# One stage for the item schedule and the projection of a graph-attention layer with a mixture-of-experts layer behind it

## What is computed

```python
xn = layernorm(x)
x_l = xn @ W_l + b_l                    # "left": rows gathered by src
x_r = xn @ W_r + b_r                    # "right": rows of the dst node
g = leaky_relu(x_r[dst] + x_l[src], 0.2)
alpha = softmax over edges of a dst of (sum_c g * att + log(edge_weight))
x = x + segment_sum(x_l[src] * alpha, dst) + bias
x = x + experts(layernorm(x))           # top 2 of 8, 256 -> 512 -> 256, gelu
```

## Time and profile before

| | us |
|---|---|
| median of 3 runs | 2044.14 |
| the profiled execution, its own time | 2046.96 |
| its span, first to last instruction | 2045.2 |
| constants | 0 to 5.1 |
| schedule | 5.1 to 111.4 |
| projection, with the start of its block | 111.4 to 224.1 |
| edges and all that follows | 224.1 to 2045.2 |

### The profile page before, as it was taken

The page is one execution under the profiler, slowest core; times in us unless marked ns, Lnnn a source line. Parts: engine busy times, 40 slices in busy tenths (PEclk is TensorE's granted clock), DMA queues, the critical chain, the costliest instruction groups (busy, mean ns, idle before and its releaser), DMA issues. The chain is left out here.

```text
span 2045.2 us, 41611 instructions
## 1 busy us (share of the span) xinstructions
PE 1732.4 (85%) x9503; PEld 1464.5 (72%) x9504; DVE 1504.5 (74%) x2831; ACT 1225.6 (60%) x3096; POOL 1236.6 (60%) x1364
## 2 busy tenths in 40 slices
PE   0079679999999999999999999998587999999960
PEld 0068457777777778778787787886486999999950
DVE  1956478988988989889899898998877333333325
ACT  0021258898988989889898898998450323333310
POOL 0457577777777767777777777771517555555520
PEclk9999789999999999999999999999658999999985
DMA  5257677777777778777787777871741222222229
GB/s 169 36 192 259 202 244 230 236 231 222 237 229 231 236 218 239 228 234 234 222 241 230 234 234 225 244 237 55 256 162 42 65 69 72 69 71 70 70 72 337
DMA packets 220914, 377.54 MB, mean 185 GB/s; under 512 B 46120, under 2 KB 104720, under 8 KB 220576
## 3 DMA queue, kind: packets, MB, share of 16 engines
q1 hardware_dynamic: 146056, 205.58, 31.0%
q0 software_dynamic: 53760, 150.08, 26.5%
q10 hardware_dynamic: 20936, 20.41, 2.9%
HBM read 321.55 MB, written 55.59 MB: 184 GB/s over the span
## 5 line engine op out<-in xcount | busy, mean ns | idle before, releaser
L713 POOL DMA_INDIRECT rows<-left_rows,idx x896 | 850.9, 950 | 314.2 <-issue 301.9
L1051 PE MATMUL p_row<-rights,hotT 128*128 128x256 f32 x1792 | 516.7, 370 | 49.2 <-DMA rows<-left_rows,idx 23.8
L1053 PE MATMUL p_row<-rows,ident 128*128 128x256 f32 x1792 | 539.8, 383 | 0.0
L1114 PE MATMUL p_gain<-W,hots 128*128 128x264 f32 x1792 | 487.1, 396 | 34.5 <-ACT W L1021 20.7
L1114 PEld LDWEIGHTS p_gain<-W,hots 128*128 128x128 f32 x1792 | 325.9, 190 | 127.3 <-issue 68.6
L1051 PEld LDWEIGHTS p_row<-rights,hotT 128*128 128x128 f32 x1792 | 329.9, 192 | 115.5 <-issue 33.1
L940 ACT ACTIVATE L<-p_row 128x512 f32<-128x512 f32 x448 | 263.3, 588 | 111.7 <-PE p_row L1053 110.5
L1010 ACT ACTIVATE far<-iota_row,dl 128x128 f32<-128x128 f32 x896 | 305.0, 391 | 0.0
L876 DVE TENSOR_TENSOR W<-rows,p_weights 128x1024 f32<-128x1024 f32 x224 | 271.7, 1213 | 42.4 <-PE p_gain L1114 41.9
L785 DVE TENSOR_TENSOR L<-L,p_weights 128x1024 f32<-128x1024 f32 x224 | 270.8, 1209 | 37.8 <-ACT L L940 33.9
L1540 ACT ACTIVATE e_hT<-e_ph,b_column 128x128 f32<-128x128 f32 x420 | 119.7, 368 | 267.6 <-PE e_ph L1565 267.6
(11 more groups left out here) (240 smaller groups left out, 1906.8 us busy)
## 6 DMA issues: line engine op xcount, KB each, us to landing
rights<-right_rows SPq DMA_DIRECT2D x448, 256.0 KB
locals<-item_locals SPq DMA_DIRECT2D x112, 256.0 KB, 3.7
rows<-left_rows,idx POOLq DMA_INDIRECT x896
right_rows<-p_parts SPq DMA_DIRECT2D x50, 256.0 KB, 2.0
c_rows<-results SPq DMA_DIRECT2D x12, 1024.0 KB, 13.4
w<-in_L_ffn_W SPq DMA_DIRECT2D x16, 512.0 KB, 6.6
left_rows<-p_y SPq DMA_DIRECT2D x50, 132.0 KB, 1.8
kept_rows<-X ACTq DMA_DIRECT2D x50, 128.0 KB, 2.0
```

The lines of the kernel that those rows point to most:

```text
L713: nc.gpsimd.indirect_dma_start(out=rows[:, g.slot(RINGS), n, :], out_offset=None, in_=d["left"][:, :], in_offset=bass.IndirectOffsetOnAxis ...
L1051: nc.tensor.matmul(to, hotT[:, g.slot(2), i, :], rights[:, g.slot(2), n, part * D:(part + 1) * D], start=(part == 0), stop=False)
L1053: last = nc.tensor.matmul(to, s["ident"][:, :], rows[:, g.slot(RINGS), i, 0:D], start=False, stop=True)
L1114: last = nc.tensor.matmul(p_gain[:, n, 0:D + H], hots[:, g.slot(2), i, :], W[:, g.slot(2), i, :, :].rearrange("p h c -> p (h c)"), start=( ...
```

## The change

`schedule` and `project` become one block, `prepare`. What it does:

- x comes on SP's queue in four pieces (tiles 0 to 6, 7 to 20, 21 to 34, 35 to 48); the block ends are read straight from the input `dst` right behind the first piece, 391 and 390 elements; ACT's queue loads `att`, weights and biases first and then copies the three edge tables to DRAM.
- Statistics, roots and reciprocals are taken by seven tiles (b = 0 to 6) and not all at once. 49 tiles are projected and not 50; the padding tile of `right` is stored as zeros.
- Normalizing moves from DVE to ACT, the copy of `left` out of PSUM too. The biases of left and right enter PSUM by a two-row matmul ahead of each product (a float32r row of ones against the high and low part of the bias), so DVE adds none. DVE takes both the high and the low part of `right` out of PSUM; POOL is left with the output bias.
- Each step of the schedule stands between two tiles of the projection, in the written order of its engine: the searches at DVE's tiles 2 to 8, the gathers behind POOL's tile 8, the steps after the gather at tiles 22 to 41.
- Rows of x are kept by seven tiles in one store on SP's queue, and not one tile at a time on ACT's.
- All loops are written out.

The added lines, cut to their core (indentation cut by twelve columns; the removed lines are the two functions printed above). In order: POOL, SP, PE, ACT, DVE.

```diff
+PIECES = ((0, BY), (BY, 3 * BY), (3 * BY, 5 * BY), (5 * BY, 7 * BY))
...
+    pool.wait_ge(weights_in, 96)
+    for t in range(NODE_TILES):
+        pool.wait_ge(normed, t + 1)
+        nc.gpsimd.tensor_tensor(X[:, t, :], X[:, t, :], bias_out[:, :], ALU.add).then_inc(residual, 1)
+        if t == 8:
+            pool.wait_ge(items_done, 1)
+            pool.wait_ge(padded, 16 * 6)
+            for q in range(QI):
+                for i, (rows, table) in enumerate(((rows_d, "dst"), (rows_s, "src"), (rows_w, "weight"))):
+                    nc.gpsimd.indirect_dma_start(
+                        out=rows[:, q, :], out_offset=None, in_=d[table][:, :],
+                        in_offset=bass.IndirectOffsetOnAxis(ap=t_idx[:, q:q + 1], axis=0),
+                    ).then_inc(gathered[i], 16)
+        if t == 26:
+            pool.wait_ge(local_done, 1)
+            nc.gpsimd.tensor_copy(local16[:, :, :], local[:, :, :]).then_inc(local_kept, 1)
...
+    def load_x(i):
+        sp.dma_start(X[:, a:own, :], x[a * P:own * P, :].rearrange("(t p) f -> p t f", p=P)).then_inc(x_in[i], 16)
+            sp.dma_start(X[0:N - full * P, full, :], x[full * P:N, :]).then_inc(x_in[i], 16)
...
+    load_x(0)
+    for i, at, blocks in ((0, 0, EB), (1, PAIR * P - 1, EB - 1)):
+        sp.dma_start(ends[:, i, 0:blocks], dst[at:at + (blocks - 1) * PAIR * P + 1][::PAIR * P]
+                     .rearrange("(a b) -> a b", a=1), allow_slow_non_contiguous=True).then_inc(ends_in, 16)
+    for i in range(1, len(PIECES)):
+        load_x(i)
+    sp.wait_ge(pads_set, 6)
+    for side in range(2):
+        sp.dma_start(d["right"][NODE_TILES * P:NT * P, side * D:(side + 1) * D], X[:, NODE_TILES, :]).then_inc(stored, 16)
+    for t in range(NODE_TILES):
+        sp.wait_ge(left_done, t + 1)
+        sp.dma_start(d["left"][t * P:(t + 1) * P, :], y[:, t % 4, :]).then_inc(tile_stored[t % 4], 16)
+        sp.wait_ge(right_done, t + 1)
+        sp.dma_start(d["right"][t * P:(t + 1) * P, :], parts[:, t % 4, :, :].rearrange("p a f -> p (a f)")
+                     ).then_inc(tile_stored[t % 4], 16)
+        if t == 12:
+            sp.wait_ge(items_done, 1)
...
+            sp.wait_ge(local_done, 2)
...
+            sp.wait_ge(stored, 16 * 5)
...
+            sp.wait_ge(local_kept, 1)
...
+        if t == 41:
+            for kind in range(MARKS):
+                sp.wait_ge(breaks_done, kind + 1)
...
+        if t % BY == BY - 1:
+            b = t // BY
+            sp.wait_ge(residual, (b + 1) * BY)
+            sp.dma_start(d["kept"][b * BY * P:(b + 1) * BY * P, :].rearrange("(t p) f -> p t f", p=P),
+                         X[:, tiles_of(b), :]).then_inc(rows_kept, 16)
+    sp.wait_ge(stored, 16 * (6 + MARKS))
+    sp.wait_ge(rows_kept, 16 * BATCHES)
+    for k in range(4):
+        sp.wait_ge(tile_stored[k], 32 * len(range(k, NODE_TILES, 4)))
...
+    def multiply(t):
+        pe.wait_ge(x_turned_copied, t + 1)
+        wait(pe, left_done, t - 1)
+        wait(pe, right_done, t - 1)
+        for side, (at, wide) in enumerate(((0, DL), (DL, D))):
+            nc.tensor.matmul(py[:, t % 2, side, 0:wide], both_ones[:, :], bias_parts[:, at:at + wide], start=True, stop=False)
+            for h in range(KD):
+                last = nc.tensor.matmul(py[:, t % 2, side, 0:wide], xT[:, t % 2, h * P:(h + 1) * P],
+                                        W[:, h, side, 0:wide], start=False, stop=(h == KD - 1))
+        last.then_inc(projected, 1)
...
+    turn(0)
+    pe.wait_ge(columns_done, 2)
+    for t in range(NODE_TILES):
+        if t + 1 < NODE_TILES:
+            turn(t + 1)
+        multiply(t)
+        if t == 1:
+            pe.wait_ge(ends_done, 1)
+            for a in range(2):
+                last = nc.tensor.matmul(ps[:, a, 0:EB], s["ones"][0:1, :], offs[0:1, a, :], start=True, stop=True)
+            last.then_inc(spread, 1)
+        i = t - 26
+        if 0 <= i < 3 * QI:
+            pe.wait_ge(local_done, 1 if i < QI else 3)
+            if i >= 2:
+                pe.wait_ge(turned_copied, i - 1)
+            if i >= 2 * QI:
+                pe.wait_ge(weights_done, 1)
+            from_ = local if i < QI else sf if i < 2 * QI else rows_w
+            nc.tensor.transpose(ps[:, i % 2, 0:P], from_[:, i % QI, :], s["ident"][:, :]).then_inc(turned, 1)
...
+    act.dma_start(attb[:, :], att.rearrange("h c -> (h c)").partition_broadcast(P)).then_inc(weights_in, 16)
+        act.dma_start(W[:, :, i, 0:D], w.rearrange("(k p) f -> p k f", p=P)).then_inc(weights_in, 16)
+    for at, b in ((0, b_l), (DL, b_r)):
+        act.dma_start(bias_rows[:, at:at + D], b.partition_broadcast(2)).then_inc(weights_in, 16)
+    act.dma_start(bias_out[:, :], bias.partition_broadcast(P)).then_inc(weights_in, 16)
+    for k, a in (("dst", dst), ("src", src), ("weight", edge_weight)):
+        act.dma_start(flat[k][0:E].rearrange("(a b) -> a b", a=16),
+                      a.rearrange("(a b) -> a b", a=16)).then_inc(padded, 16)
...
+    def norm(t):
+        act.wait_ge(scaled, t // BY + 1)
...
+        nc.scalar.activation(xn[:, t % 2, :], X[:, t, :], ACT.Identity, bias=shift[:, t:t + 1],
+                             scale=std[:, 2, t:t + 1]).then_inc(normed, 1)
...
+    def copy_left(t):
+        act.wait_ge(projected, t + 1)
+        wait(act, tile_stored[t % 4], 32 * (t // 4))
+        nc.scalar.activation(y[:, t % 4, :], py[:, t % 2, 0, 0:DL], ACT.Copy).then_inc(left_done, 1)
+    root(0)
+    for t in range(-2, NODE_TILES):
+        if t + 2 < NODE_TILES:
+            norm(t + 2)
+        if 0 <= t + 1 < NODE_TILES:
+            copy_turned(t + 1)
+        if t >= 0:
+            copy_left(t)
+        if (t + 4) % BY == 0 and 0 < t + 4 < NODE_TILES:
+            root((t + 4) // BY)
+        if t == 31:
+            act.wait_ge(floored, 1)
+            nc.scalar.activation(rows_w[:, :, :], rows_w[:, :, :], ACT.Ln).then_inc(logged, 1)
+        i = t - 27
+        if 0 <= i < 3 * QI:
+            act.wait_ge(turned, i + 1)
+            to = (s["dl"], s["srcs"], s["logw"])[i // QI][:, (i % QI) * P:(i % QI + 1) * P]
+            nc.scalar.activation(to, ps[:, i % 2, 0:P], ACT.Copy).then_inc(turned_copied, 1)
...
+    def take_stats(b):
+        for i, (a, z) in enumerate(PIECES):
+            if a <= b * BY < z:
+                v.wait_ge(x_in[i], 32 if z > full else 16)
...
+        nc.vector.tensor_scalar(std[:, 0, tiles_of(b)], mv[:, tiles_of(b), 1], EPS, None, ALU.add).then_inc(sqrt_ready, 1)
...
+    def scale(b):
+        v.wait_ge(sqrt_done, b + 1)
+        step(nc.vector.reciprocal(std[:, 2, tiles_of(b)], std[:, 1, tiles_of(b)]))
+        nc.vector.scalar_tensor_tensor(shift[:, tiles_of(b)], mv[:, tiles_of(b), 0], -1.0, std[:, 2, tiles_of(b)],
...
+    def take_parts(t):
+        v.wait_ge(projected, t + 1)
+        wait(v, tile_stored[t % 4], 32 * (t // 4))
+        right = py[:, t % 2, 1, 0:D]
+        nc.vector.tensor_scalar(parts[:, t % 4, 0, :].bitcast(I32), right.bitcast(I32),
+                                LOW_BITS, LOW_BITS, ALU.logical_shift_right, ALU.logical_shift_left).then_inc(right_high, 1)
+        v.wait_ge(right_high, t + 1)
+        nc.vector.tensor_tensor(parts[:, t % 4, 1, :], right, parts[:, t % 4, 0, :], ALU.subtract).then_inc(right_done, 1)
...
+    take_stats(0)
+    take_moments(0)
+    v.wait_ge(weights_in, 96)
+    by_head = attb[:, :].rearrange("p (h c) -> p h c", c=C)
...
+    scale(0)
+    nc.vector.tensor_scalar(both_ones[:, :], s["iota"][0:2, :], 0.0, 1.0, ALU.mult, ALU.add).then_inc(columns_done, 1)
...
+    nc.vector.scalar_tensor_tensor(bias_parts[:, :], bias_high[:, :], s["ident"][0:2, 0:1], bias_low[:, :],
+                                   ALU.mult, ALU.add).then_inc(columns_done, 1)
...
+    v.wait_ge(ends_in, 32)
...
+    nc.vector.tensor_tensor(offs[:, 1, 1:EB], count[:, 1:EB], count[:, 0:EB - 1], ALU.subtract
+                            ).then_inc(ends_done, 1)
+    take_stats(1)
+    take_moments(1)
+    for t in range(NODE_TILES):
+        b = (t + 3) // BY
+        if (t + 3) % BY == 0 and b < BATCHES:
+            scale(b)
+        take_parts(t)
+        b = (t + 6) // BY
+        if (t + 6) % BY == 0 and 2 <= b < BATCHES:
+            take_stats(b)
+        b = (t + 5) // BY
+        if (t + 5) % BY == 0 and 2 <= b < BATCHES:
+            take_moments(b)
+        if t == 1:
+            v.wait_ge(spread, 1)
+            for a in range(2):
+                step(nc.vector.tensor_copy(offs_all[:, a, :], ps[:, a, 0:EB]))
+            v.wait_ge(numbered, 1)
+            step(nc.vector.tensor_scalar(number_i[:, 1, :], number_i[:, 0, :], 1, None, ALU.logical_shift_right))
+            step(nc.vector.tensor_copy(number[:, :], number_i[:, 0, :]))
+            step(nc.vector.tensor_copy(pair[:, :], number_i[:, 1, :]))
+            step(nc.vector.scalar_tensor_tensor(half[:, :], pair[:, :], -float(PAIR), number[:, :], ALU.mult, ALU.add))
+        if 2 <= t < 2 + QI:
+            find(t - 2)
+        if t == 1 + QI:
...
```

(42 more changed lines are left out.)

358 lines of the change are left out of this document (112 added, 246 removed).

## The result

The changed kernel takes 2021.71 us (2019.49 to 2023.44, 4 runs), the kernel before on the same chip 2044.10 (2042.96 to 2045.32, 4 runs): 22.4 us less, ratio 0.989 with a 95% interval of 0.9873 to 0.9907. 2001 was forecast, with a range to 2017. The direction was right, the size half of what I expected, and the result lies above the range.

A forecast was written before the change was run, and what follows sets the result against it. Bound by waits and single chains up to 111 us, then PE. Overlapping the two moves the edge stage's first issue from 224.1 to 181, 43 us less: 2044.14 - 43 = 2001 us, range 1985 to 2017.

The forecast's parts named there:

- Part 1, the load: Start of the fused stage, loading x, weights and block ends: the ends come last, at 25 us, range 14 to 33.
- Part 2: Until the first tile: DVE's chain over the block ends 4.7 us, statistics and aggregates 3.1; DVE reaches its loop at 33.
- Part 3, DVE-bound until 61: Tiles 0 to 8, bound by DVE: the loop sums to 27.8 us, items done at 61 against 66.3 before.
- Part 4, POOL's order: POOL's gathers delay output bias and stores, so PE stops after tile 19 at 84.4 and resumes at 98.2, 14 us idle.
- Part 5, the pace: Projection bound by PE at 2.26 us a tile, bounds 2.02 and 2.50, bias matmuls 0.12 each; tiles 20 to 48 take 65.5.
- The steps that don't fit: Tiles 20 to 48: DVE's long steps, PE's squares and ACT's logarithm exceed PE's cover, 7.0 us together, bounds 2.5 and 14.
- Part 6, the tail: After the last product: DVE's parts 0.9, last kept store 6.5 (4.5 to 8.8), 0.9 to the edge stage's first issue at 181.
- the gap of PE of 10 to 15 us: Expected sign: PE idle between about 84 and 98 us, granted clock down behind it; its absence would show the forecast wrong.
- C: Rival: pace of 2.8 us a tile because ACT has three operations a tile in one order with PE; 2017 us, chance 0.12.
- A: Rival: POOL's gathers don't stop the pipeline, PE goes on at 84.4 without the restart; 15.8 us less, 1985, chance 0.13.
- B: Rival: late start, dear block ends or x's pieces holding ACT's issues; DVE enters its loop at 43 to 45; 2012, chance 0.16.
- D: Rival: PE stays at its low clock, 4.4 us a tile, slower than before by 33 us; 2077, chance 0.03.

## Why the prediction was wrong

**What bounds the kernel, and the plan:** right. No barrier is left, the schedule hides beside the projection, and PE is the bound from there on.

**Part 1, the load:** right in the end, wrong in what comes last. DVE used the ends without a wait at 22.57 (25 forecast), because by then its own work was last: the weighted columns ended at 19.0 and the bias's two rows at 22.6. The second of the two issues was through at 16.60 (5.62 + 10.98). The ends had landed by 22.57, so 12.5 + 10.6 + 2 was at least 2.4 too long; when each of them landed the profile doesn't show, so the split isn't tested. The first piece of x was there at 12.63 (12.5 forecast), though 242 GB/s was no upper bound: the earlier trace rows itself has 263, and from 20 to 40 us the changed kernel moved 302.

**Part 2:** DVE's loop began at 30.79, 33 forecast.

**Part 3, DVE-bound until 61:** wrong by two terms. The items were done at 67.8, and the loop took 37.0 us in place of 27.8. The first term is the pace: PE, mostly at its lower level, needed 5.7 us for tile 1 (with the spreading matmul) and 5.5 for tile 2 (transposes at 28.27, 33.95 and 39.44), and DVE waited for it (6.7 us in three waits); from tile 4 on DVE worked at 3.1 a tile and waited no more. The second the sum left out: it put the statistics of the third seven tiles behind the searches, but in the code of the change they stand ahead of the last one, and so ahead of the items:

```profile
62.06 2.38 DVE L503 BATCH_NORM_STATS2 stats<-X 128x6 f32<-128x256 f32 x7
```

27.8, 6.7 and 2.4 make 36.9. With 128 rows the gathers began at 61.95 on one chip and 61.08 on the other, beside the 61 forecast, but that is partly luck: on the first of these the loop took 30.8 us, with the 2.4 in it, and had begun at 30.85, two microseconds before the forecast. (That the nine tiles cost some 10 us against a projection alone doesn't follow from its numbers either: 61 - 33 - 20 is 8. The sum doesn't use it.)

**Part 4, POOL's order:** the chain was right, link by link, and its size was not. It counted on a PE that would run out of work at 84.4. In the changed kernel PE got to the end of tile 19 at 99.9 and lost 3.65 us. The kept store landed so that ACT went on after 5.0 us (97.67 to 102.62; 6 taken). With 128 rows the kept store was issued at 91.56 (90.7 forecast), which agrees with POOL's part of the chain. The rest isn't tested there. PE went on at 92.71, after standing 8.9 us and another 6 earlier, but what it stood for was DVE's wait for the buffers of tile 10, which ended before tile 14's stores were even issued:

```profile
91.56 0.37 SPq L393 DMA_DIRECT2D kept_rows<-X  x1
91.78 0.42 DVE L530 TENSOR_SCALAR p_parts<-p_py 128x256 int32<-128x256 int32 x1 [15.37 <-remote]
92.19 0.36 SPq L357 DMA_DIRECT2D left_rows<-p_y  x1
```

So that stop is the one of late stores, and no run shows what the written order alone would cost a PE at 2.22 a tile. The restart cost 2.0 in the sum; tile 20's two sides took 5.57 from transposes to transposes (103.55 to 109.12) against 2.99, so 2.6.

The Trainium skill ("TensorE: Matmul & The Clock Gate", section "A second HAM failure mode: psum-queue depth-cycling") tells of a clock that goes up and down where the engine idles briefly between groups. The trace agrees for two of the three stretches at 0.50: they begin at waits of PE, 2.73 us for DVE (to 68.69) and 3.65 (to 103.55). It doesn't for the first, ahead of which PE shows no wait from 22.7 to 34. My sum counted one restart; the first two cost nothing behind tile 20, whose start hung on the gathers.

**Part 5, the pace:** this is the step that failed. "a float32r one about 0.12, and 0.24 is its upper bound": measured, the pair cost 0.97 a tile and not 0.24, and the upper bound of 2.50 a tile was passed by 0.49. The price was taken from the earlier trace rows, where float32r matmuls stand between others of 128 rows, and there it holds: 0.12 each with 128 rows. The term that was missing is what the neighbours lose when an operand of two rows comes between them. I had no row with such an operand, and took the columns for the whole cost, and my upper bound changed only the number of passes. It should have allowed for a weight load that nothing overlaps.
The Trainium skill (the same page, section "LDWEIGHTS (loading the stationary operand)") says that a weight load takes as long for 32 rows as for 128. The trace agrees, 0.18 for two rows and 0.19 for 128, but the time of the load isn't its cost: whether it runs beside the matmul ahead of it is.

The steps that don't fit, 7.0 forecast, came to 3.4: from the restart at 103.55 to the last product's end at 196.3 it is 92.75 us, less 2.6 for the low clock and 29 x 2.99. A slower PE covers more of DVE's long steps: once the clock is up again, the longest two spacings are 3.60 and 3.54 here, 0.6 and 0.4 over their neighbours, and 6.18 and 4.62 with 128 rows, 4.0 and 2.3 over. The squares cost 0.11 a tile (3.10 for 2.99; 0.12 forecast). That work on POOL, ACT and DVE beside PE costs nothing was right: ACT waited for PE 46 times.

**Part 6, the tail:** 6.1 from the last product (196.3) to the edge stage, 8.3 forecast. The kept store landed in 4.4 on the median, where the forecast had 6.5 between 4.5 and 8.8. From the DMA issues of the page:

```profile
kept_rows<-X SPq DMA_DIRECT2D x7, 896.0 KB, 4.4
```

**The sum.** Tile 20 starts 5.4 late (103.55 for 98.2: the items are 6.8 late, and the steps behind them are some 1.5 quicker than taken); the pace adds 29 x 0.73 = 21.2, the clock 0.6; the long steps give back 3.6 and the tail 2.2. Together 21.4, the whole miss of the stage. One of the signs that I had set down for being wrong came: the gap of PE of 10 to 15 us isn't there. The stretch behind the first edge DMA is 1815.4 us and not 1821, within what single executions differ.

**The rivals.** C came nearest in number (2.8 a tile, 2017) and had the wrong cause. A's condition didn't hold: the gathers stood ahead of tile 14's stores. That PE stopped for only 3.65 us came of its slower pace, and brought none of A's gain. B didn't happen. D's 4.4 a tile was passed wherever the clock was low (5.5 for tile 2), but only in stretches of 10 us or less; the fp32 form alone stayed at the low level. The range ended at C, and C's 2.8 was itself below what was measured.

## What to carry to other kernels

A small matmul set between large ones is to be priced by what it does to the weight loads around it, not by its columns: give it as many rows as its neighbours, with zeros, or put all the small ones together. When an engine becomes the bound in a fused stage, a surcharge per tile counts once for each tile behind the last stop, so it deserves its own measurement before a stop of 14 us does. And a step is priced where the code has it: DVE's 2.4 us of statistics were counted behind the searches and stood among them. And a stop that is worked out for a fast engine shrinks when the engine turns out slower: the two terms must not be summed as if they were independent.

## What the runs showed of the hardware

- At full clock, a matmul with a float32r operand of two or 32 rows between 128-row ones costs 0.38 us of PE beyond the 0.12 that it takes with 128 rows, 126 of them zero (0.77 a tile for two apart, 0.38 for two in one group). The weight load at a change of the row count begins only with its own matmul.
- A two-row fp32 pair in each tile left PE at its lower clock for the whole projection, at 6.81 us a tile, while the float32r form reached the higher one.
- Chips differ in their indirect DMAs: ahead of the same 896 gathers of the same kernel POOL was idle 793 us against 307, and stores issued beside the 21 gathers seem to land only behind them there (tile 10's, issued at 68, released its buffer after 95).
